# The tanh form of GELU written out: a hyperbolic tangent on ScalarE, a square on GpSimd, two products on VectorE

## What is computed

```
ff = jax.nn.gelu(h @ W1 + b1, approximate=False) @ W2 + b2               # layer 0: exact
h = jax.nn.gelu(h @ fc1_w + fc1_b, approximate=True) @ fc2_w + fc2_b     # layer 1: tanh form
h2 = jax.nn.gelu(h2 @ w1) @ w2                                           # layer 2: tanh form (the default)
h = jax.nn.gelu(u @ w1 + b1, approximate=False)                          # layer 3, masked MLPs: exact
h = jax.nn.gelu(ff_norm @ ff_w1 + ff_b1, approximate=True)               # layer 3, last MLP: tanh form
```

## Time and profile before

| what | us |
|---|---|
| median of 3 runs (lowest, highest) | 471.72 (468.32 to 473.46) |
| the profiled execution | 472.36 |
| its span, first to last instruction | 470.3 |
| busy: TensorE, VectorE, ScalarE, GpSimd | 402.6, 342.7, 332.4, 146.0 |
| last attention half's last Exp pair ends | 434.3 |

### The profile page before, as it was taken

The page is one execution under the profiler, slowest core; times in us unless marked ns, Lnnn a source line. Parts: engine busy times, 40 slices in busy tenths (PEclk is TensorE's granted clock), DMA queues, the critical chain, the costliest instruction groups (busy, mean ns, idle before and its releaser), DMA issues.

```text
span 470.3 us, 9898 instructions
## 1 busy us (share of the span) xinstructions
PE 402.6 (86%) x3658; PEld 207.3 (44%) x3661; DVE 342.7 (73%) x639; ACT 332.4 (71%) x626; POOL 146.0 (31%) x211
## 2 busy tenths in 40 slices
PE   2588888679998999998999889998999898897886
PEld 2353334244544444544545444445444445453554
DVE  5279998768983989875898939898768998321422
ACT  1605777487777886877868778868787797998532
...
GB/s 227 163 301 47 102 3 2 1 2 5 1 3 136 2 2 5 2 101 36 2 5 3 2 136 0 6 2 2 96 42 3 1 2 14 2 13 1 2 11 11
DMA packets 15583, 17.60 MB, mean 37 GB/s; under 512 B 2268, under 2 KB 14366, under 8 KB 15520
## 3 DMA queue, kind: packets, MB, share of 16 engines
...
## 4 chain that ended last, share of the span: by engine, by line
PE 49%; DVE 23%; ACT 13%; issue 9%; POOL 3%; SPq 2%; DMA 1%; ACTq 0%; DVEq 0%; POOLq 0%
DVE mx L1083 14%; PE pv_ps L822 13%; ACT probs L918 7%; PE max_ps L639 6%; PE max_ps L768 6%; PE exp_ps L648 6%; PE exp_ps L755 6%; PE pv_ps L624 3%; DVE xhat L1012 2%; PE exp_ps L689 2%; PE exp_ps L614 2%; DVE mparts L1075 1%; PE max_ps L614 1%; ACT L897 1%; SPq L558 1%
## 5 line engine op out<-in xcount | busy, mean ns | idle before, releaser
L918 ACT ACTIVATE probs<-exp_ps 128x512 f32<-128x512 f32 x384 | 204.4, 597 | 70.4 <-PE exp_ps L648 70.0
L1083 DVE TENSOR_REDUCE mx<-max_ps 128x2 f32<-128x1024 f32 x192 | 228.3, 1217 | 19.5 <-PE max_ps L639 19.0
L648 PE MATMUL exp_ps<-q_stack,k_stack 64*128 64x256 bf16 x768 | 123.4, 274 | 16.8 <-ACT probs L918 14.8
L639 PE MATMUL max_ps<-k_stack,q_stack 64*128 64x512 bf16 x384 | 103.8, 396 | 20.2 <-DVE mx L1083 12.9
L822 PE MATMUL pv_ps<-probs,v_ones 128*32 128x256 f32 x1536 | 104.5, 389 | 2.1 <-ACT probs L918 0.8
L1103 POOL TENSOR_TENSOR rstd<-var_eps,half 128x2 f32<-128x2 f32 (+1 forms) x30 | 21.8, 726 | 237.4 <-DVE var_eps L956 237.3
L648 PEld LDWEIGHTS exp_ps<-q_stack,k_stack 64*128 64x128 bf16 x768 | 42.1, 94 | 88.4 <-ACT probs L918 54.5
L822 PEld LDWEIGHTS pv_ps<-probs,v_ones 128*32 128x32 f32 x1536 | 41.5, 109 | 36.4 <-ACT probs L918 9.9
L639 PEld LDWEIGHTS max_ps<-k_stack,q_stack 64*128 64x128 bf16 x384 | 29.9, 94 | 45.9 <-DVE mx L1083 28.5
L755 PE MATMUL exp_ps<-hT,w 128*128 128x256 f32 x128 | 38.0, 409 | 3.5 <-ACT hT L854 1.4
L897 ACT ACTIVATE hid<-exp_ps,vec 128x256 f32<-128x256 f32 x64 | 28.1, 473 | 9.6 <-PE exp_ps L755 8.9
...
## 6 DMA issues: line engine op xcount, KB each, us to landing
...
q_stack<-mrows SPq DMA_DIRECT2D x48, 4.0 KB
...
```

The lines of the kernel that those rows point to most:

```text
L639: return pe.matmul(max_bank(n + j), half(q_stack, b, pair, j)[:, t * P:(t + 1) * P], half(k_stack, b, pair, j), start=True, stop=True)
L648: return pe.matmul(exp_bank(e)[:, of_two * HALF:(of_two + 1) * HALF], half(k_stack, b, pair, j)[:, kt * P:(kt + 1) * P], half(q_stack, b, ...
L918: act.activation(probs[:, tile % RING_P, :], exp_bank(e), ACT.Exp, scale=SCORE_SCALE[hc // 2 // NB]).then_inc(exp_read, 1)
L1083: dve.tensor_reduce(mx[:, G % 2, t, 2 * (pair % 2):2 * (pair % 2) + 2], max_ps[:, n % MAX_BANKS:n % MAX_BANKS + 2, :], AX_X, ALU.max, nega ...
```

## The change

GELU's tanh form is computed in five steps for every MLP that has it, except those of job 7's second half. ScalarE writes r = c u into `hid` with Identity, c being the root of 0.044715 (its biases are multiplied by c once, `vec_root`). GpSimd squares two chunks at a time (r squared, 128 by 512). VectorE makes (r squared + 1) r in one instruction (item CUBE), ScalarE takes the tanh of it (TANH), VectorE makes (tanh + 1) r (GELU), and the factor 1/(2c) goes into the addition behind W2. So a W1 has two CUBE, two TANH and two GELU items (two chunks each), a W1F one of each. These bursts have no HOLD. The lists get new gaps, `TANH_0` and `TANH_1` are the lists of jobs 4 and 5, `FOLD_LAG` becomes 6, and W2 waits for `hid_done` instead of for the activations. There are 10 such bursts: W1 of jobs 4, 5, 6 (both halves) and 7 (first half), and W1F of jobs 6 (both halves) and 7 (first half).

```diff
-FOLD_LAG = 5
+FOLD_LAG = 6
-FIRST_JOB = [("ST", 1), ("XH", 6), ("TR", 2), ("K", 1), ("Q", 3), ("SQ", 0), ("DK", 1), ("DK", 0), ("DK", 2), ("DQ", 0),
+FIRST_JOB = [("ST", 1), ("XH", 5), ("TR", 2), ("K", 1), ("Q", 4), ("SQ", 0), ("DK", 1), ("DK", 0), ("DK", 2), ("DQ", 0),
...
+TANH_0 = [("OT", 2), ("WO", 0), ("SX", 1), ("XH", 3), ("TR", 1), ("W1", 0), ("W1", 1), ("W1", 0), ("W1", 1), ("CUBE", 1),
+          ("CUBE", 0), ("TANH", 1), ("TANH", 0), ("GELU", 1), ("GELU", 2), ("W2", 2), ("SX", 1), ("XH", 1), ("TR", 1),
+          ("K", 1), ("Q", 1), ("RK", 1), ("RQ", 2), ("SQ", 1)]
+TANH_1 = [("OT", 0), ("ZQ", 1), ("WO", 0), ("SX", 1), ("XH", 2), ("TR", 2), ("W1", 0), ("W1", 1), ("W1", 0), ("W1", 1),
+          ("CUBE", 3), ("CUBE", 0), ("TANH", 0), ("TANH", 0), ("GELU", 1), ("GELU", 1), ("W2", 1), ("SX", 1), ("XH", 2),
+          ("TR", 1), ("K", 1), ("Q", 1), ("RK", 1), ("RQ", 0), ("V", 0), ("SQ", 1), ("DK", 0), ("DK", 0), ("DK", 1),
+          ("DQ", 1), ("DQ", 0), ("DQ", 0)]
+LAST_0 = [("OT", 2), ("WO", 0), ("SX", 2), ("XH", 2), ("TR", 2), ("W1", 0), ("W1", 1), ("W1", 0), ("W1", 1), ("CUBE", 1),
+          ("CUBE", 0), ("TANH", 1), ("TANH", 0), ("GELU", 1), ("GELU", 1), ("W2", 2), ("SX", 2), ("XH", 4), ("TR", 1),
+          ("MK", 0), ("HOLD", 2), ("W1S", 0), ("W1S", 1), ("W2S", 1), ("SX", 1), ("XH", 2), ("TR", 2), ("W1F", 0),
+          ("W1F", 2), ("CUBE", 1), ("TANH", 1), ("GELU", 1), ("W2F", 2)]
+LAST_1 = [("OT", 2), ("WO", 0), ("SX", 1), ("XH", 2), ("TR", 3), ("W1", 0), ("W1", 1), ("W1", 0), ("W1", 1), ("CUBE", 1),
+          ("CUBE", 0), ("TANH", 1), ("TANH", 2), ("GELU", 1), ("GELU", 1), ("W2", 0), ("SX", 2), ("XH", 4), ("TR", 1),
+          ("MK", 1), ("HOLD", 0), ("W1S", 0), ("W1S", 1), ("W2S", 2), ("SX", 3), ("XH", 3), ("TR", 2), ("W1F", 0),
+          ("W1F", 2), ("CUBE", 1), ("TANH", 1), ("GELU", 1), ("W2F", 1)]
+END_0 = [("OT", 3), ("WO", 1), ("SX", 1), ("XH", 2), ("TR", 1), ("W1", 0), ("W1", 1), ("W1", 0), ("W1", 1), ("CUBE", 1),
+         ("CUBE", 0), ("TANH", 1), ("TANH", 0), ("GELU", 1), ("GELU", 1), ("W2", 2), ("SX", 4), ("XH", 4), ("TR", 1),
+         ("MK", 1), ("HOLD", 0), ("W1S", 0), ("W1S", 2), ("W2S", 2), ("SX", 0), ("XH", 2), ("TR", 2), ("W1F", 0),
+         ("W1F", 2), ("CUBE", 0), ("TANH", 1), ("GELU", 1), ("W2F", 1)]
+END_1 = [("OT", 1), ("WO", 0), ("SX", 4), ("XH", 2), ("TR", 2), ("W1", 0), ("W1", 1), ("W1", 0), ("W1", 0), ("W2", 1),
+         ("SX", 2), ("XH", 2), ("TR", 1), ("MK", 0), ("W1S", 0), ("W1S", 3), ("W2S", 0), ("SX", 0), ("XH", 2), ("TR", 1),
+         ("W1F", 1), ("W1F", 3), ("W2F", 1)]
+ROOT = 0.044715 ** 0.5
+TANH_SCALE = (2 / np.pi) ** 0.5 / ROOT
+TWO_ROOTS = 2 * ROOT
...
 CHUNKS = {"W1": 4, "W1S": 2, "W1F": 2}
...
+def by_tanh(name, k, h):
+
+    return (k, h) != (LAST, 1) and (name[2:] == "F" or (name[2:] == "" and k >= 2 * NB))
...
     if k < NB:
         return FIRST_JOB
+    if k < 2 * NB:
+        return (MID_0, MID_1)[h]
     if k < CHAINS:
-        return (MID_0, MID_1)[h]
+        return (TANH_0, TANH_1)[h]
     return (LAST_0, LAST_1)[h] if k < LAST else (END_0, END_1)[h]
...
-                            if tt == 0:
+                            if tt == 0 and by_tanh(name, k, h):
+                                pe.wait_ge(hid_done, GELU_NO[k, h, 2 if name == "W2F" else j // 2] + 1)
+                            elif tt == 0:
                                 pe.wait_ge(*read_by_act(("W1" + name[2:], k, h, j)))
...
+                elif name in CHUNKS and by_tanh(name, k, h):
+
+                    n = EXP_USE[item]
+                    col = hidden_bias(name, layer)
+                    bias = vec_root[:, V_ZERO:V_ZERO + 1] if col is None else vec_root[:, col + c:col + c + 1]
+                    act.wait_ge(bias_set, 1)
+                    act.wait_ge(exp_full, n + 1)
+                    act.activation(hid[:, c, cols], exp_bank(n)[:, 0:HALF], ACT.Identity, bias=bias, scale=ROOT).then_inc(exp_read, 1)
+                elif name == "TANH":
+                    j = chunks_by_tanh(c)[1]
+                    act.wait_ge(cubed, CUBE_NO[k, h, c] + 1)
+                    act.activation(cube[:, j:j + 2, cols], cube[:, j:j + 2, cols], ACT.Tanh, scale=TANH_SCALE).then_inc(tanh_done, 1)
...
+                    dve.tensor_scalar(vec_root[:, :], vec[:, :], ROOT, None, ALU.mult).then_inc(bias_set, 1)
...
+                elif name == "CUBE":
+
+                    j = chunks_by_tanh(c)[1]
+                    dve.wait_ge(squared, SQUARE_NO[k, h, c] + 1)
+                    dve.scalar_tensor_tensor(out=cube[:, j:j + 2, cols], in0=cube[:, j:j + 2, cols], scalar=1.0, in1=hid[:, j:j + 2, cols],
+                                             op0=ALU.add, op1=ALU.mult).then_inc(cubed, 1)
+                elif name == "GELU":
+                    j = chunks_by_tanh(c)[1]
+                    dve.wait_ge(tanh_done, TANH_NO[k, h, c] + 1)
+                    dve.scalar_tensor_tensor(out=hid[:, j:j + 2, cols], in0=cube[:, j:j + 2, cols], scalar=1.0, in1=hid[:, j:j + 2, cols],
+                                             op0=ALU.add, op1=ALU.mult).then_inc(hid_done, 1)
...
+                    elif name != "WO" and by_tanh(name, k, h):
+                        ins = dve.scalar_tensor_tensor(out=x[:, b, own], in0=src, scalar=1 / TWO_ROOTS, in1=(xg if gated else x)[:, b, own],
+                                                       op0=ALU.mult, op1=ALU.add)
...
+                elif name in CHUNKS and by_tanh(name, k, h) and c % 2 == 1:
+                    pool.wait_ge(*read_by_act(item))
+                    pool.tensor_tensor(cube[:, c - 1:c + 1, cols], hid[:, c - 1:c + 1, cols], hid[:, c - 1:c + 1, cols], ALU.mult).then_inc(squared, 1)
```

30 lines of the change are left out of this document (15 added, 15 removed).

## The result

The changed kernel takes 483.89 us in the median (480.37 to 485.82, 4 runs) against 470.73 (468.32 to 473.46, 4 runs) for the kernel before; the ratio is 1.027, with an interval of 1.018 to 1.036. Its profiled execution is the shortest of its four, 480.37 us with a span of 478.6 and a mean granted TensorE clock of 0.971; the other three took 483.09 to 485.82 us with a clock of 0.961 to 0.954. The forecast was 478 for the median, with a range of 463 to 487, and 478.3 for the span. As a change of the median it was +6.3 us (from 471.7), and +13.2 was measured (from 470.73).

A forecast was written before the change was run, and what follows sets the result against it. An interlock of three engines, ScalarE with most air, was taken to bound the kernel. Bursts -17.5, hole +10.7, empty beats +2.3, stalls +4.5 and tail +8 gave +8.0: span 478.3, median 479.7, shaded to 478; range 463 to 487.

The forecast's parts named there:

- one empty beat: A single beat without Exp (119 and 193 in the plan), costing a max beat's 1.13 us each, +2.3 together.
- W1F -4.4: Job 6's second W1F burst moves behind the last Exp, saving 3.45 us and its W2F about 1.0.
- W2 -1.95: W2 of job 7's first half moves behind the end of the exp lane, saving 1.95 us.
- stalls +4.5: VectorE and TensorE both near 96% in the stretch with layer 2's maxima; waits between 0 and +5.5 us, taken as +4.5.
- What bounds the kernel: Whole kernel: an interlock of three engines, TensorE 86% busy, VectorE 73%, ScalarE 71%, with ScalarE having the most air.
- Rival 3: ScalarE was the limit in the bursts after all, so its net 10 us comes off too: some 457 us; chance 0.05.
- Part 1, the held bursts: TensorE fills held bursts, table loads lie beside; seven unheld W1 bursts save 1.6 us each, -17.5 with end moves.
- Part 2, the hole: Between layer 1's and layer 2's attention, beats 152 to 160 have no exp: 16.7 us bound by VectorE, net +10.7.
- Rival 1, the cheap hole: The hole takes 11 us, net +5, without stalls and with tail +5: 466.5 us; chance 0.25.
- Part 3, VectorE and GpSimd: 34 new products at 0.69 us add 23.5 to VectorE; GpSimd's squares, 1.27 each, cost nothing; stalls +4.5.
- rival 4: Collision: a third of the 34 products wait half of 1.27 us for a square or split, 7 us: 486; chance 0.10.
- Part 4, the tail: Behind the last Exp: OT at 8.3 us instead of 3.6, job 7's halves interleaved differently; +8, a tail of 44.

The follow-up runs named there:

- e1: The kernel before with only the three list and lag edits that have nothing to do with GELU (FIRST_JOB, MID_0, FOLD_LAG); 469.07 us, ratio 0.9933.
- e2: The kernel before with ScalarE's Tanh in place of the tanh-form Gelu in the ten bursts, holds and lists kept, rest of the formula left out; 469.87 us.
- e3: e2 with the holds of those ten bursts also taken out of the plan, nothing else; 494.95 us, ratio 1.0474 to the kernel before.
- e4: The changed kernel with built-in GELU, holds and MID lists in jobs 4 and 5, the formula kept in jobs 6 and 7; 471.75 us, ratio 0.9973.
- e9: The changed kernel with built-in GELU, its holds and the MID lists in job 4 alone; 488.14 us, ratio 1.0347.
- e12: The changed kernel with three gaps of the list TANH_1 cut, so the plan's empty exp stretch is five beats instead of nine; 487.33 us, ratio 1.0325.
- e14: The changed kernel with three unread TensorE products ahead of each of five max beats in the hole; 483.21 us, ratio 1.0217.
- e6: The changed kernel with VectorE's 34 new products cut to 2 columns instead of 512; 474.65 us, ratio 1.005.
- e5: The changed kernel with GpSimd's 17 squares replaced by memsets of the same tiles, which read nothing; 482.57 us, ratio 1.0206.
- e7: The changed kernel with built-in GELU, holds and earlier END lists for job 7 and W1F of job 6's second half; 488.23 us, ratio 1.0317.
- e10: The changed kernel with the formula only in job 6 (both W1, first half's W1F), built-in GELU, holds and earlier lists elsewhere; 476.59 us, ratio 1.0078.

## Why the prediction came out right, point by point

The span was forecast at 478.3 and is 478.6 in the profiled execution, the median at 478.0 and is 483.9; 483.9 is inside the range, and slower was the likeliest sign. The sum came out so close because errors cancelled, and because the profiled execution was the fastest of the four: by the medians the change is +13.2, twice the +6.3 forecast. So the sign and the range were right, and the tenths were luck. Against e1, by stretches:

| stretch | predicted | measured |
|---|---|---|
| the lists that don't touch GELU | 0 | -3.6 |
| up to half 5's first Exp | 0 | -0.6 |
| halves 5 to 8: four bursts -6.4, hole +10.7, one empty beat +1.1 | +5.4 | +9.6 |
| halves 9 to 11: three bursts -4.8, W1F -4.4, W2 -1.95, one empty beat +1.1, stalls +4.5 | -5.5 | -3.8 |
| tail | +8 | +6.8 |
| sum | +8 | +8.3 |

(Measured: the difference of the spans of e1 and before; the first Exp of half 5 at 203.6 less 204.2; the sums of the halves, 137.7 less 128.1 and 93.3 less 97.1; the tails, 42.84 less 36.06. Rounding leaves 0.1. The stalls are put whole into the third stretch.)

**What bounds the kernel.** Right: an interlock in which ScalarE has air. e2 takes 19.5 us off ScalarE's busy time (332.4 to 312.9) and gets 2.7. Rival 3 is out.

**Part 1, the held bursts.** The reading that the loads lie beside TensorE's work was right. The size, -1.6 for each burst without hold, was too much where the hold alone goes. The empty beats that a hold gives have a use, since the max lane moves on in them. In e3, which changes nothing but the holds, job 4's two bursts give 1.5 together (halves 5 and 6, clock 1.00) instead of 3.2, job 5's nothing, and the empty beats come back as a hole. In the kernel after, halves 5 and 6 are 3.6 shorter than in e1, more than forecast (3.2 less 1.1 for the empty beat); but part of that is moved work, as TR to RQ of job 4's second half stand in half 6's beats in e1 (137 to 140) and in half 7's here (139 to 143). One unheld burst, read in ScalarE's timeline:

```profile
218.36 1.09 ACT L972 ACTIVATE probs<-exp_ps 128x512 f32<-128x512 f32 x2
...
230.45 1.08 ACT L972 ACTIVATE probs<-exp_ps 128x512 f32<-128x512 f32 x2 [0.89 <-PE exp_ps L688]
...
234.18 1.09 ACT L972 ACTIVATE probs<-exp_ps 128x512 f32<-128x512 f32 x2 [2.16 <-PE exp_ps L688]
```

These are seven exp beats, 15.82 us. Less 7 times 1.285 and one empty beat of 1.13, the burst cost 5.7, not the 4.07 of its products, and as much as the 5.66 of a held one. For halves 9 to 11 the forecast was -11.2 for the bursts of jobs 6 and 7, +1.1 for an empty beat and +4.5 for stalls, -5.5 in sum; e4 against e1 gives -4.8. The sum is near, and what each term gave is not shown.

**Part 2, the hole.** Right in place, cause and size: 17.7 us for 16.7, VectorE busy 92% of it. e4 removes it, e9 moves it, e12 shortens it with the plan (6.4 for four beats), and in e14 keeping the clock up with more TensorE work doesn't shorten it. Rival 1, the cheap hole, fell. The net, +10.7, was too low, but it can't be read apart from the bursts: halves 5 to 8 grew by 9.6 in sum, for +5.4. With the forecast's own -6.4 for four bursts and +1.1 for the empty beat the hole's net is 14.9; with e3's 0.7 a burst it is 11.3. By these two, between 2.8 and 6.4 of the 17.7 us came back, where 6 were forecast.

**Part 3, VectorE and GpSimd.** The products' medians are 0.68, the means 0.74 and 0.71 for the assumed 0.69. The squares took 1.04 instead of 1.27. e6 prices the products at 6.1 us by spans and 9.2 by medians, which is more than the +4.5 of stalls. The two full engines I argued with are there. For the stretch with layer 2's maxima, less the hole, I expected VectorE busy 95.2 of 103.5 us, 92%. In the kernel after it runs from the hole's end to the last max reduction, and its first 46 us stand below it:

```profile
311.00:413.90 102.90, 90.55 (x909) 45.85 (x906) 92.24 (x160) 77.38 (x158) 28.61 (x42) 1.00 0.07 17
311.00:357.00 46.00, 41.89 (x439) 20.56 (x440) 42.34 (x68) 35.25 (x74) 15.26 (x24) 1.00 0.14 37
```

That is 90% over the whole and 92% in its first part, beside TensorE's 88% and 91%. Without the products, in e6, the same stretch takes 99.0 us (309.3 to 408.3, VectorE busy 85.83), 3.9 less, near the +4.5. So the forecast of this part held; which wait the products lengthen is not shown. The other 2 us or more lie outside it, most of them in half 6.

The Trainium skill (SBUF — State Buffer, Who interferes with whom) has a VectorE instruction with two SBUF inputs and a GpSimd instruction that reads SBUF exclude one another. The trace agrees where they meet, but they seldom do. Of the 34 products only one ran beside a square, the first pair below, from the kernel after; the second pair is the same product in e5, beside a memset:

```profile
438.57 1.04 POOL L1290 TENSOR_TENSOR cube<-hid 128x512 f32<-128x512 f32 x1 [3.59 <-ACT hid L937]
439.04 1.11 DVE L1111 SCALAR_TENSOR_TENSOR hid<-cube,hid 128x512 f32<-128x512 f32 x1 [1.61 <-ACT cube L941]
...
440.97 0.52 POOL L1290 MEMSET cube<- 128x512 f32 x1 [4.10 <-ACT hid L937]
441.47 0.69 DVE L1111 SCALAR_TENSOR_TENSOR hid<-cube,hid 128x512 f32<-128x512 f32 x1 [1.61 <-ACT cube L941]
```

Three more products took 0.88, 0.88 and 1.27 us in the kernel after, beside other GpSimd work (two splits, one gate product); the other 30 took 0.68 to 0.69. All four together lost 1.4 us, not the 7 of rival 4: a square is done before its own product starts, and the plan rarely puts another burst's product beside it.

**Part 4, the tail.** OT was forecast at 8.3 behind the last Exp and stands at 8.4, in TensorE's timeline of the kernel after:

```profile
444.12 0.38 PE L770 MATMUL exp_ps<-ident,o_tok 128*128 128x128 f32 x2
```

The last Exp ends at 435.73 (forecast 434.5) and the tail is 42.9 (44). The size was right. Of its terms OT's delay came true, but e7 and e10 put OT back to 3.5 and keep at least some 3.5 us of a longer tail, for which the clock gives no account. What seems to count is how much of job 7's first half is done when the last Exp is: by the plans, whatever shortens the exp lane leaves more of it for the tail, and the holds had given it time. That is argued; no run tests it alone.

**What I had not counted.** The lists that don't touch GELU (-3.6), which my sum left out, and TensorE's clock, below. The clock goes along with the 3.5 us by which the median stands above the profiled execution: in the three longer executions it was 0.01 to 0.017 lower, and e7's profile has the place, 3.5 us more at the lower level at the hole and halves 7 and 8 2.2 us longer.

No kernel with the formula beats e1. The best version found is the kernel before with the list edits of e1, 0.9933.
